# Two-layer GNN on one core: the float32 copy of hn moves from VectorE to ScalarE

## The chip, the cores and the metric

The kernel runs on one core of a Trainium2 chip. The metric is the device time of one execution in microseconds (us). The time before is 2117.98 us, the median of 3 runs (2113.94 to 2120.04).

## The reference, cut to what matters

128 independent graphs, each with features x of 128 nodes x 512 and a 128 x 128 adjacency matrix, go through two layers:

```
# layer 0, per graph
h = relu(layernorm(x));  A = adj + I;  d = rowsum(A) ** -0.5
x = x + (d A d) @ (h @ W + b)
# layer 1, per graph;  H = (adj != 0), Be = 1 / (nodes of each edge), Dn = 1 / (H @ w), w = first row of adj
xh = relu(layernorm(x))
h  = relu(Dn * (H @ (Be * (H^T @ (xh @ W1^T)))) + b1)       # 128 x 1024
hn = layernorm(h) * gamma + beta
x  = x + xh + Dn * (H @ (Be * (H^T @ (hn @ W2^T)))) + b2
```

## The kernel before, in words

Every product is done in float16 with a split: a float32 value v becomes hi = float16(v) and lo = float16(v - hi), and three matmuls (hi x hi, hi x lo, lo x hi) are added up in PSUM. Aggregation over nodes is done before the product with the weights, so each graph has five such pieces on TensorE: T0 (h0 with A), Y0 (with W), T1 (xh with P, where P = H Be H^T), Y1 in two halves of 512 columns (with W1), T2 (hn with P) and Y2 (with W2).

The work is a software pipeline written out by hand. Each engine has its own instruction stream, and `every_step` runs `step(i, k)` for k = -3 to 130; in step k an engine works on pieces of up to six neighbouring graphs (a = k, b_ = k-1, c = k-2, o = k-3, p = k+1, e = k+2). Steps 6 to 123 are a hardware loop that holds two steps in its body, so one step of two has the jump back behind it. The order within an engine is the order of the code; between engines semaphores are waited on. Most tiles have one buffer, some have two by the parity of the graph.

TensorE's order in a step: the row sums, Y1's second half (line 314, ps_c, graph c), T0 (L303 to L305, graph a; it waits for h0_hi and h0_lo), Y2 (L314, ps_y, graph o; waits for t2h and t2l), deg, T1 (graph b_), Y0, P, T2 (L303 to L305, ps_t, graph c; waits for hn_hi and hn_lo), Y1's first half (graph b_; waits for t1h and t1l), and the transpose of the next adjacency matrix.

The second layer norm of graph c: VectorE makes z from Y1's halves (L598, two instructions; the second is called z1 below), ScalarE makes h = relu(z) (L460), VectorE takes bn_stats (L603) and bn_aggr (L708), and GpSimd turns these into a scale sc2 and a bias nm2 (L930, L935, L938). Then:

```
L475 ScalarE:  hn_hi = Identity(h * sc2 + nm2)   (float16), waits for nm2
L763 VectorE:  hn    = h * sc2 + nm2             (float32), waits for nm2
L777 VectorE:  hn_lo = hn - hn_hi,                waits for both
```

ScalarE's hn_hi stands at the top of its following step, and behind it t1h (L480), which waits for T1. On VectorE hn is followed by HB_lo (L767), hn_lo (L777), out_t (L786, the finished output of graph o), t1l (L791), two tiny instructions, and the next step begins with x1 (L619). Later in that next step comes raw0 (L642, bn_stats of the next x_t, which waits for its load), t2l, the first z, u (L667), h0_lo (L673) and z1.

SyncE's queue in a step: the load of adj_t, then the store of out_t (it waits for out_t), and behind that the load of x_t for graph a+2, which raw0 of the next step reads.

GpSimd, behind nm2 (L938), goes on with base0 (L845, 128x512), qdn (L852), dn2 and dn1 (L860, L867), bias0 (L872), and scr2 (L878, 128x512, the sum of x1b and xh), and none of these waits for hn.

Of the kernel before, what the change touches and what calls it, by code (L numbers as in the profile page):

```python
# [5 lines left out]
def bass_adjacency_prenorm_two_layer_gnn_kernel(  # L6
# [24 lines left out]
    ALU = mybir.AluOpType  # L31
    ACT = mybir.ActivationFunctionType
# [30 lines left out]
    with ctx:  # L63
        def sb(name, shape, dt=F32):
            return ctx.enter_context(nc.sbuf_tensor(name, shape, dt))

        def sem(name):
            return ctx.enter_context(nc.semaphore(name))
# [58 lines left out]
        z, h = sb("z", [128, DH]), sb("h", [128, DH])  # L127
        raw2, st2 = sb("raw2", [128, NCH, 6]), sb("st2", [128, 2, 2])
        u2, sc2, nm2 = sb("u2", [128, 1]), sb("sc2", [128, 2]), sb("nm2", [128, 2])
        hn = sb("hn", [128, DH])  # L130
# [68 lines left out]
        s_h = [sem(f"h_chunk{c}_ready") for c in range(NCH)]  # L199
        s_rw2 = [sem(f"bn_raw2_chunk{c}_ready") for c in range(NCH)]  # L200
        s_stat2 = sem("stats2_ready")
        s_u2, s_pp2, s_ln2 = sem("ln2_var_eps"), sem("ln2_rstd"), sem("ln2_scalars_ready")
        s_hn, s_hnh, s_hnl = sem("hn_ready"), sem("hn_hi_ready"), sem("hn_lo_ready")
# [4 lines left out]
        def live(g, i):  # L208
            return not isinstance(i, int) or 0 <= g < NG
# [4 lines left out]
        def wait(eng, s, i, g):  # L214

            if not isinstance(i, int) or g >= 0:
                eng.wait_ge(s, i + (g + 1 if not isinstance(i, int) else min(g + 1, NG)))
# [212 lines left out]
        def _(act):  # L430
# [36 lines left out]
            def step(i, k):  # L467
                e, a, b_, c, o = k + 2, k, k - 1, k - 2, k - 3
                if live(o, i):
                    m = o % 2  # L470
                    wait(act, s_ln2, i, o)
                    wait(act, s_h[0], i, o)
                    wait(act, s_h[1], i, o)
                    wait(act, s_t2, i, o - 1)
                    act.activation(hn_hi[:, :], h[:, :], ACT.Identity, bias=nm2[:, m:m + 1], scale=sc2[:, m:m + 1])\  # L475
                       .then_inc(s_hnh, 1)
                if live(c, i):
                    wait(act, s_t1, i, c)
                    wait(act, s_y1[NCH - 1], i, c - 1)
                    act.activation(t1h[:, :], T1[:, :], ACT.Copy, scale=T1_EVAC).then_inc(s_t1h, 1)  # L480
# [12 lines left out]
                if live(b_, i):  # L493
                    m = b_ % 2
# [8 lines left out]
                if live(a, i):  # L503
                    m = a % 2
# [4 lines left out]
                                   scale=rd0[:, m, 0:1]).then_inc(s_h0, 1)  # L509
# [4 lines left out]
                                   scale=rd0[:, m, 0:1]).then_inc(s_h0h, 1)  # L514
# [12 lines left out]
                if live(b_, i):  # L527
                    m = b_ % 2
# [10 lines left out]
                if live(a, i):  # L539
                    m = a % 2  # L540
# [8 lines left out]
                if live(e, i):  # L549
                    m = e % 2  # L550
# [6 lines left out]
                if at_step(i, k, 2):  # L557
                    beta_term(0, 0)

            every_step(ENG.Activation, step)  # L560


        @block.vector
        def _(dve):
# [45 lines left out]
            def step(i, k):  # L610
                e, p, a, b_, c, o = k + 2, k + 1, k, k - 1, k - 2, k - 3
                if live(b_, i):
                    m = b_ % 2
# [7 lines left out]
                if live(p, i):  # L621
                    m = p % 2
# [6 lines left out]
                if live(p, i):  # L629
                    m = p % 2  # L630
# [9 lines left out]
                if live(p, i):  # L640
                    wait_dma(dve, s_x, i, p)
                    dve.bn_stats(raw0[:, :], x_t[:, p % 2, :]).then_inc(s_rw0, 1)  # L642
                    m = p % 2
# [19 lines left out]
                if live(p, i):  # L663
                    m = p % 2
# [15 lines left out]
                if live(b_, i):  # L680
                    m = b_ % 2
# [3 lines left out]
                if live(a, i):  # L685
                    wait(dve, s_cm, i, a)
                    dve.reciprocal(inv_t[:, :], cm[:, :]).then_inc(s_bi, 1)
                    m = a % 2
# [52 lines left out]
                if live(b_, i):  # L741
                    m = b_ % 2
# [6 lines left out]
                if live(a, i):  # L749
                    m = a % 2  # L750
# [3 lines left out]
                if live(e, i):  # L754
                    m = e % 2
# [1 line left out]
                    wait(dve, s_ahat, i, e)  # L757
                    wait(dve, s_t0, i, e - 2)
                    dve.tensor_tensor(A_lo[:, m, :], ahat[:, :], A_hi[:, m, :], ALU.subtract).then_inc(s_al, 1)
                if live(c, i):  # L760
                    m = c % 2
                    wait(dve, s_ln2, i, c)
                    dve.tensor_scalar(hn[:, :], h[:, :], sc2[:, m:m + 1], nm2[:, m:m + 1], ALU.mult, ALU.add).then_inc(s_hn, 1)  # L763
                if live(a, i):
                    m = a % 2
                    wait(dve, s_hbh, i, a)
# [13 lines left out]
                if live(o, i):  # L780
                    m = o % 2
# [11 lines left out]
                if live(e, i):  # L793
                    m = e % 2
# [5 lines left out]
                if live(p, i):  # L800
                    m = p % 2
                    wait(dve, s_ht, i, p)
                    dve.tensor_scalar(cm[:, :], cnt[:, m:m + 1], 1.0, 1.0 / P_SCALE, ALU.max, ALU.mult).then_inc(s_cm, 1)

            every_step(ENG.DVE, step)


# [168 lines left out]
```

## Time and profile before

| | us |
|---|---|
| median of 3 runs | 2117.98 |
| the profiled execution | 2120.77 |
| its span, first to last instruction | 2119.0 |
| TensorE busy (matmul) | 2066.9 |
| VectorE busy | 1852.1 |
| GpSimd busy | 1448.8 |
| ScalarE busy | 1203.7 |
| hn_hi on ScalarE, L475, mean of one | 1.241 |
| hn on VectorE, L763, mean of one | 1.287 |
| hn_lo on VectorE, L777, mean of one | 1.219 |

The span is one execution; busy times of the engines overlap. A group's mean says nothing of when its instructions run; for that the timeline is read. Start times are counted from the span's start. The granted TensorE clock had a mean of 0.995.

### The profile page before, as it was taken

The numbers are of one execution on the slowest core, as the hardware profiler recorded it, in microseconds if no ns is written. First come the engines' busy times: TensorE is split into PE (matmuls) and PEld (weight loads), VectorE is DVE, ScalarE is ACT, GpSimd is POOL, SyncE is SP. The second block draws the span as 40 slices with busy tenths as digits, with TensorE's granted clock in tenths as the row PEclk, the third lists the DMA queues.
The fourth block names the chain that finished last, engine by engine and source line by source line (L and its number), as shares of the span: only waits on it lengthen the run. The fifth ranks groups of instructions, "written<-read, shape, count | busy, mean of one in ns | idle before, by whom it ended". The sixth has DMA issues, their size and how long they took to land.

```text
span 2119.0 us, 52979 instructions
## 1 busy us (share of the span) xinstructions
PE 2066.9 (98%) x14614; PEld 1139.8 (54%) x14614; DVE 1852.1 (87%) x4514; ACT 1203.7 (57%) x2225; POOL 1448.8 (68%) x2318
## 2 busy tenths in 40 slices
PE   4899999999999999999999999999999999999998
PEld 2455555555555555555555555555555555555554
DVE  5989889888889988888888888888898898888875
ACT  6555555555555555555555555555555555555553
POOL 3667667767767767776776676776677677667663
PEclk9999999999999999999999999999999999999999
DMA  4011111110111111111111111111111111111100
GB/s 147 30 34 35 43 33 35 43 33 35 40 37 35 35 41 33 35 43 33 35 43 33 35 40 37 33 35 43 33 35 43 33 35 43 34 35 37 39 27 21
DMA packets 58346, 82.13 MB, mean 39 GB/s; under 512 B 6736, under 2 KB 23120, under 8 KB 58320
## 3 DMA queue, kind: packets, MB, share of 16 engines
q1 hardware_dynamic: 58320, 81.82, 11.9%
q8 instruction: 11, 0.18, 0.0%
q14 instruction: 15, 0.12, 0.0%
HBM read 48.24 MB, written 33.55 MB: 39 GB/s over the span
## 4 chain that ended last, share of the span: by engine, by line
PE 95%; issue 2%; DVE 1%; DMA 1%; POOL 1%; ACT 0%; SPq 0%; DVEq 0%; POOLq 0%
PE ps_c L314 46%; PE ps_y L314 31%; PE ps_c L303 3%; PE ps_c L304 3%; PE ps_c L305 3%; PE ps_t L303 3%; PE ps_t L304 3%; PE ps_t L305 3%; PE ps_a L424 1%; DMA adj_t<-in_adj_dram 0%; PE ps_p L397 0%; PE ps_p L396 0%; PE ps_y L332 0%; DMA raw_w<-in_W_dram 0%; DVE raw L603 0%
## 5 line engine op out<-in xcount | busy, mean ns | idle before, releaser
L908 POOL TENSOR_TENSOR rd<-u,neg_half 128x2 f32<-128x2 f32 x128 | 137.8, 1077 | 227.6 <-DVE u L667 227.6
L498 ACT ACTIVATE P_hi<-ps_p 128x128 f16<-128x128 f32 x128 | 35.4, 277 | 441.2 <-PE ps_t L305 433.2
L460 ACT ACTIVATE h<-z 128x512 f32<-128x512 f32 x256 | 161.3, 630 | 192.3 <-DVE z L598 192.0
L314 PE MATMUL ps_c<-w1l,t1h 128*128 128x512 f16 x1024 | 263.4, 380 | 0.0
L314 PE MATMUL ps_c<-w1h,t1h 128*128 128x512 f16 x1024 | 263.3, 379 | 0.0
L314 PE MATMUL ps_c<-w1h,t1l 128*128 128x512 f16 x1024 | 262.8, 379 | 0.0
L475 ACT ACTIVATE hn_hi<-h,nm,sc 128x1024 f16<-128x1024 f32 x128 | 158.8, 1241 | 172.0 <-POOL nm L938 171.9
L314 PE MATMUL ps_y<-w2h,t2h 128*128 128x512 f16 x1024 | 243.3, 381 | 2.4 <-issue 2.4
L598 DVE SCALAR_TENSOR_TENSOR z<-ps_c,dn,b_all 128x512 f32<-128x512 f32 x256 | 188.2, 735 | 62.8 <-PE ps_c L314 62.3
L314 PE MATMUL ps_y<-w2l,t2h 128*128 128x512 f16 x1024 | 242.3, 379 | 0.0
L891 POOL TENSOR_TENSOR x1b<-x,b_all 128x512 f32<-128x512 f32 x128 | 162.6, 1270 | 116.0 <-DVE x L619 116.0
L314 PE MATMUL ps_y<-w2h,t2l 128*128 128x512 f16 x1024 | 241.9, 379 | 0.0
L930 POOL TENSOR_SCALAR u<-st 128x1 f32<-128x1 f32 x128 | 92.9, 726 | 174.9 <-DVE st L708 174.8
L845 POOL TENSOR_TENSOR base<-scr,x_t 128x512 f32<-128x512 f32 x128 | 182.6, 1426 | 27.0 <-issue 22.4
L763 DVE TENSOR_SCALAR hn<-h,sc,nm 128x1024 f32<-128x1024 f32 x128 | 164.7, 1287 | 25.1 <-POOL nm L938 25.1
L303 PE MATMUL ps_t<-P_hi,hn_hi 128*128 128x128 f16 x1024 | 178.2, 219 | 4.9 <-issue 4.2
L305 PE MATMUL ps_t<-P_hi,hn_lo 128*128 128x128 f16 x1024 | 178.3, 219 | 0.0
L304 PE MATMUL ps_t<-P_lo,hn_hi 128*128 128x128 f16 x1024 | 178.3, 219 | 0.0
L826 POOL TENSOR_TENSOR base<-scr,vq 128x512 f32<-128x512 f32 x128 | 162.8, 1272 | 11.4 <-ACT vq L454 11.4
L314 PEld LDWEIGHTS ps_c<-w1l,t1h 128*128 128x128 f16 x1024 | 100.3, 98 | 121.5 <-issue 1.1
L314 PEld LDWEIGHTS ps_y<-w2l,t2h 128*128 128x128 f16 x1024 | 100.4, 98 | 121.4 <-issue 1.1
L314 PEld LDWEIGHTS ps_c<-w1h,t1l 128*128 128x128 f16 x1024 | 100.2, 98 | 121.0 <-issue 0.3
(133 smaller groups left out, 5774.1 us busy)
## 6 DMA issues: line engine op xcount, KB each, us to landing
x_t<-in_x_dram SPq DMA_DIRECT2D x128, 256.0 KB, 2.7
out_dram<-out_t SPq DMA_DIRECT2D x128, 256.0 KB, 2.0
adj_t<-in_adj_dram SPq DMA_DIRECT2D x128, 64.0 KB, 1.8
raw_w<-in_W1T_dram SPq DMA_DIRECT2D x4, 512.0 KB, 7.6
raw_w<-in_W2T_dram SPq DMA_DIRECT2D x8, 256.0 KB, 8.8
raw_w<-in_W_dram SPq DMA_DIRECT2D x4, 256.0 KB, 3.7
b_all<-in_b_dram SPq DMA_DIRECT2D x2, 256.0 KB, 6.9
b_all<-in_b_dram SPq DMA_DIRECT2D x1, 512.0 KB, 10.3
```

Of the source, the lines that this page charges most:

```text
L303: pe.matmul(ps[:, f], lhs_hi[:, f], rhs_hi, start=True, stop=False)
L304: pe.matmul(ps[:, f], lhs_hi[:, f], rhs_lo, start=False, stop=False)
L305: mm = pe.matmul(ps[:, f], lhs_lo[:, f], rhs_hi, start=False, stop=True)
L314: mm = pe.matmul(ps, t[:, j * 128:(j + 1) * 128], w[:, j, cols], start=(n == 0 and j == 0), stop=(n == 2 and j == blocks - 1))
L460: act.activation(h[:, cols], z[:, cols], ACT.Relu).then_inc(s_h[n], 1)
L475: act.activation(hn_hi[:, :], h[:, :], ACT.Identity, bias=nm2[:, m:m + 1], scale=sc2[:, m:m + 1])\
L598: dve.scalar_tensor_tensor(out=z[:, cols], in0=Y1[n][:, :], scalar=dn1[:, m:m + 1], in1=b1_all[:, cols], op0=ALU.mult, op1=ALU.add).then_i ...
L763: dve.tensor_scalar(hn[:, :], h[:, :], sc2[:, m:m + 1], nm2[:, m:m + 1], ALU.mult, ALU.add).then_inc(s_hn, 1)
L826: pool.tensor_tensor(base2[:, m, :], scr2[:, m, :], vq[:, :], ALU.add).then_inc(s_base2, 1)
L845: pool.tensor_tensor(base0[:, :], scr0[:, :], x_t[:, a % 2, :], ALU.add).then_inc(s_base0, 1)
L891: pool.tensor_tensor(x1b[:, :], x1[:, a % 2, :], b2_all[:, :], ALU.add).then_inc(s_x1b, 1)
L908: pool.tensor_tensor(rd0[:, m, :], u0[:, m, :], neg_half[:, :], ALU.pow).then_inc(s_pp0, 1)
```

## The change

The VectorE instruction for hn is taken out. ScalarE makes hn with the same function, scale and bias as hn_hi, as one more instruction right behind hn_hi. It has the waits of hn_hi, but for the last: where hn_hi waits for T2 of the graph before, hn waits for hn_lo of the graph before, the reader of the single buffer. Everything else keeps its order.

```diff
@@ ScalarE, top of the step @@
                     act.activation(hn_hi[:, :], h[:, :], ACT.Identity, bias=nm2[:, m:m + 1], scale=sc2[:, m:m + 1])\
                        .then_inc(s_hnh, 1)
+                    wait(act, s_ln2, i, o)
+                    wait(act, s_h[0], i, o)
+                    wait(act, s_h[1], i, o)
+                    wait(act, s_hnl, i, o - 1)
+                    act.activation(hn[:, :], h[:, :], ACT.Identity, bias=nm2[:, m:m + 1], scale=sc2[:, m:m + 1])\
+                       .then_inc(s_hn, 1)
                 if live(c, i):
                     wait(act, s_t1, i, c)
@@ VectorE, behind A_lo @@
-                if live(c, i):
-                    m = c % 2
-                    wait(dve, s_ln2, i, c)
-                    dve.tensor_scalar(hn[:, :], h[:, :], sc2[:, m:m + 1], nm2[:, m:m + 1], ALU.mult, ALU.add).then_inc(s_hn, 1)
                 if live(a, i):
                     m = a % 2
                     wait(dve, s_hbh, i, a)
```

## Rows read from the trace of the kernel before

**Rows 1.** The page, part 1: busy us (share of the span) and instructions.
```profile
PE 2066.9 (98%) x14614; PEld 1139.8 (54%) x14614; DVE 1852.1 (87%) x4514; ACT 1203.7 (57%) x2225; POOL 1448.8 (68%) x2318
```

**Rows 2.** Windows from one step's T0 to another's, 119 steps on: length, busy.
```profile
106.52:2013.44 1906.92, 1903.88 (x13567) 1051.82 (x13566) 1703.62 (x4165) 1094.49 (x2023) 1342.53 (x2142) 1.00 0.11 37
```

**Rows 3.** Timeline of TensorE: start, length in us; first matmuls of T0 and T2.
```profile
1004.10 0.22 PE L303 MATMUL ps_c<-A_hi,h_hi 128*128 128x128 f16 x1
...
1013.34 0.22 PE L303 MATMUL ps_t<-P_hi,hn_hi 128*128 128x128 f16 x1
...
1020.02 0.22 PE L303 MATMUL ps_c<-A_hi,h_hi 128*128 128x128 f16 x1
...
1036.03 0.22 PE L303 MATMUL ps_c<-A_hi,h_hi 128*128 128x128 f16 x1
```

**Rows 4.** Waits: who waited for whom, us in total, times, longest.
```profile
DVE raw L642 <- DMA x_t<-in_x_dram: 56.1, 68, 1.1
```

**Rows 5.** Timeline of VectorE over two steps; idle before in brackets.
```profile
1004.05 0.75 DVE L598 SCALAR_TENSOR_TENSOR z<-ps_c,dn,b_all 128x512 f32<-128x512 f32 x1 [0.21 <-PE ps_c L314]
...
1008.85 1.74 DVE L763 TENSOR_SCALAR hn<-h,sc,nm 128x1024 f32<-128x1024 f32 x1 [0.17 <-POOL nm L938]
...
1010.79 1.21 DVE L777 TENSOR_TENSOR hn_lo<-hn,hn_hi 128x1024 f16<-128x1024 f32 x1
...
1020.23 0.75 DVE L598 SCALAR_TENSOR_TENSOR z<-ps_c,dn,b_all 128x512 f32<-128x512 f32 x1 [0.72 <-PE ps_c L314]
...
1027.04 1.21 DVE L777 TENSOR_TENSOR hn_lo<-hn,hn_hi 128x1024 f16<-128x1024 f32 x1
1028.17 0.74 DVE L786 SCALAR_TENSOR_TENSOR out_t<-ps_y,dn,base 128x512 f32<-128x512 f32 x1
...
1032.36 0.69 DVE L642 BATCH_NORM_STATS2 raw<-x_t 128x6 f32<-128x512 f32 x1 [0.78 <-DMA x_t<-in_x_dram]
...
1035.08 0.69 DVE L673 TENSOR_TENSOR h_lo<-h,h_hi 128x512 f16<-128x512 f32 x1
```

**Rows 6.** Timeline of SyncE's queue: the two loads of x_t.
```profile
1013.43 0.33 SPq L246 DMA_DIRECT2D x_t<-in_x_dram  x1
...
1029.78 0.33 SPq L246 DMA_DIRECT2D x_t<-in_x_dram  x1
```

**Rows 7.** The page, part 6: issues, KB each, median us to landing.
```profile
x_t<-in_x_dram SPq DMA_DIRECT2D x128, 256.0 KB, 2.7
```

**Rows 8.** Timeline of ScalarE in these steps, and one row near the end.
```profile
1008.93 1.24 ACT L475 ACTIVATE hn_hi<-h,nm,sc 128x1024 f16<-128x1024 f32 x1 [1.36 <-POOL nm L938]
...
1016.10 0.81 ACT L508 ACTIVATE h<-x_t,bias,rd 128x512 f32<-128x512 f32 x1
1016.81 0.81 ACT L513 ACTIVATE h_hi<-x_t,bias,rd 128x512 f16<-128x512 f32 x1
...
1025.02 1.24 ACT L475 ACTIVATE hn_hi<-h,nm,sc 128x1024 f16<-128x1024 f32 x1 [1.28 <-POOL nm L938]
...
2087.45 1.24 ACT L475 ACTIVATE hn_hi<-h,nm,sc 128x1024 f16<-128x1024 f32 x1 [2.65 <-POOL nm L938]
```

**Rows 9.** Timeline of GpSimd in these steps, and one row near the end.
```profile
1008.78 1.26 POOL L845 TENSOR_TENSOR base<-scr,x_t 128x512 f32<-128x512 f32 x1
...
1025.37 1.60 POOL L845 TENSOR_TENSOR base<-scr,x_t 128x512 f32<-128x512 f32 x1 [0.38 <-issue]
1027.06 1.32 POOL L852 TENSOR_SCALAR qdn<-q,dn 128x1 f32<-128x1 f32 x1
...
1028.99 1.27 POOL L878 TENSOR_TENSOR scr<-x1b,xh 128x512 f32<-128x512 f32 x1
...
2088.67 1.26 POOL L878 TENSOR_TENSOR scr<-x1b,xh 128x512 f32<-128x512 f32 x1
```

**Rows 10.** One line of the program, L852: duration ns min/median/max.
```profile
L852 POOL TENSOR_SCALAR qdn<-q,dn x128: 288/590/1323, 43.4 to 2087.5; 128x1 f32<-128x1 f32 x128
```

**Rows 11.** Timeline of VectorE near the end, beside the last rows of 8 and 9.
```profile
2088.78 2.24 DVE L777 TENSOR_TENSOR hn_lo<-hn,hn_hi 128x1024 f16<-128x1024 f32 x1 [0.52 <-ACT hn_hi L475]
```

## The prediction

> **What bounds the kernel now.** I read the busy times first: TensorE 98%, VectorE 87%, ScalarE 57% [rows 1]. That says "TensorE", but not how near VectorE stands behind it. So next the steps: 119 of them take 1906.92 us [rows 2], 16.02 each, 32.05 for two. In the timeline T0 starts at 1004.10, 1020.02 and 1036.03 [rows 3]: 15.92 is what TensorE needs for a step with nothing to wait for, 9.24 of it from T0 to T2 and 6.68 from T2 to the next T0. Only about 0.1 us a step is lost. The loss sits at T0: in the second step h0_lo ends at 1035.77 and T0 starts 0.27 later, while z1, which needs only the matmuls ahead of T0, starts 0.21 behind T0 where T0 isn't held (1020.23 against 1020.02) [rows 3, 5].
>
> Why is h0_lo late? VectorE waits for x_t ahead of raw0 in every second step (68 waits) [rows 4], and x_t is loaded behind the store of out_t, and out_t stands behind hn_lo. The chain from one step to the next, in the second step: z1 1020.23, hn_lo 1027.04 to 1028.25, out_t to 1028.91 (+0.66), issue of x_t 1029.78 (+0.87; +0.77 in the first step, 1013.43), raw0 1032.36, h0_lo to 1035.77 (+3.41), T0 1036.03 [rows 3, 5, 6]. Landing takes 2.7 in the median [rows 7]. So hn_lo, which the change touches, already stands on the path that sets T0, with almost no slack. I call the step of 1008 A and that of 1025 B; they alternate.
>
> **The change part by part.**
>
> Removed: hn on VectorE, which took 1.74 in A (it stood behind base0, which started at 1008.78 and ended at 1010.04) [rows 5, 9]. The time freed is ahead of hn_lo, and VectorE has nothing to put there but HB_lo, so it turns into waiting for ScalarE. Worth nothing by itself.
>
> Added: a second pass on ScalarE. No row has Identity with a float32 result at this size; the same form with float32 and with float16 results takes 0.81 both ways and the second starts 0.71 after the first [rows 8], so I take 1.24 as for hn_hi, 0.10 of it overlapped. Bounds: 0.81 (as a 512-wide one) and 1.5. VectorE starts 0.09 after ScalarE's end (2087.45 + 1.24 = 2088.69, then 2088.78) [rows 8, 11]. So hn_lo can start in A at 1008.93 + 1.14 + 1.24 + 0.08 = 1011.39 (was 1010.79, +0.60), in B at 1025.02 + 2.46 = 1027.48 (was 1027.04, +0.44) [rows 5, 8]. The waits added are met by then. Behind hn on ScalarE stands t1h, some 0.4 to 0.5 later than before; its reader t1l stands two VectorE instructions behind hn_lo, which is later still, so that costs nothing.
>
> Moved by that, the large term: hn_lo meets scr2 on GpSimd. Near the end, scr2 started at 2088.67 and hn_lo at 2088.78, and hn_lo took 2.24 instead of 1.21: it ended 1.09 after scr2's end [rows 9, 11]. The reverse is seen as well: qdn took 1.32 beside hn_lo in B [rows 5, 9] and 0.29 where nothing is beside it [rows 10]. So the two exclude each other, and the first to start wins. Where does scr2 stand in the changed kernel? In A base0 ends at 1010.04, qdn starts 0.10 later and now needs 0.29 (hn_lo is not yet there): 1010.43. From qdn's end to scr2's start B shows 0.61 (1028.38 to 1028.99). So scr2 starts at 1011.04, or up to 0.09 later if HB_lo gets in ahead of base0; hn_lo comes at 1011.39, 0.26 to 0.35 too late, and ends 1.09 behind scr2's end at about 1012.36: 1013.45 instead of 1012.00. In B base0 starts 0.38 later (the jump back): 1025.37 + 1.26 + 0.09 + 0.29 + 0.61 = 1027.62 for scr2, and hn_lo comes at 1027.48, ahead of it by 0.14, with bias0 in front for a moment; I take its end at 1028.75 (was 1028.25).
>
> The steps then, counted from z1's start. A: hn_lo ends 9.40 after z1 (1013.45 - 1004.05); +0.66 +0.77 +2.70 +3.41 puts h0_lo's end at 16.93. VectorE's z1 of the next step stands behind it: 16.86. T0 of B is at 16.93 + 0.27 = 17.20, 0.34 behind its z1. B: hn_lo ends at 8.52; +0.66 +0.87 +2.70 +3.41 = 16.16, T0 could start at 16.43; TensorE itself allows z1 at 0.34 + 15.92 + 0.21 = 16.47, which is later. Pair: 16.86 + 16.47 = 33.33 against 32.05, +1.28. T2 waits too in A (natural 9.20, hn_lo ready 9.66), but the longer chain covers it. 59.5 pairs give +76; the last graph, with no work beside it, adds the second pass, 1.1. On the profiled execution: 2120.8 + 77 = 2198. That execution is 2.8 above the median of the runs, so 2195.
>
> A rule about those ports: the Trainium skill, "SBUF — State Buffer", "Who interferes with whom", has the shared pair of VectorE and GpSimd as a lock held for the whole instruction by the one that issues first. The 2.24 us agrees. For nm2 it makes a difference: HB_lo now follows A_lo directly, while nm2 runs. By the page nm2, issued first, isn't held and the sum stays; qdn's median of 0.59 over its 0.29 [rows 10] says that a tiny GpSimd instruction can lose 0.30 beside HB_lo. If nm2 loses 0.25 in each step, A's chain is longer by that: +15 us, 2210. I keep it inside the range.
>
> **The rivals.**
>
> 1. No collision: hn_lo starts ahead of scr2 in both steps (the second pass shorter by 0.3, or GpSimd's small instructions slower). Then only +0.60 and +0.44 remain: h0_lo + 0.27 at 16.36 after z1 in both, plus 15.92 + 0.21 back to z1: 32.47 to 32.49 a pair, +0.43, 26 us with the end: 2144. Against it: the 0.26 to 0.35 margin in A is a sum of rows.
>
> 2. Collision in both: B's margin of 0.14 fails. hn_lo ends at 1027.62 + 1.27 + 1.09 = 1029.98, 9.75 after z1; h0_lo ends at 17.39, z1 of the next A at 17.32: 34.18 a pair, +2.13, 127 us: 2245.
>
> 3. Faster: VectorE at 87% is the near bottleneck, it loses 1.29 us a step (mean of L763), and T0's waits vanish. The 1906.92 become 119 x 15.92 = 1894.5, 12 us less: 2106. It is decided where h0_lo is bound by VectorE's queue and not by x_t's load; it would need hn ready by 1010.79, a second pass of under 0.7 us. Rows 4 and the 0.78 wait at 1032.36 [rows 5] speak against it. The Trainium skill, "Perfetto Trace Analysis", "Optimizing Scalar/DVE Operations", says that moving work to ScalarE may make sense if VectorE is saturated; that rule would give this rival. The trace shows it short of saturated where it counts: it waits.
>
> 4. No change: the delay of hn_lo is swallowed, because out_t's store or the load has slack that the chain of waits hides: 2112 to 2124. For it: in A raw0 shows no wait for x_t. Against it: B does, in nearly every pair.
>
> **How the numbers follow.** Collision in A alone 0.62 (own range 2175 to 2216, for landings of 2.6 to 2.8, nm2's 0.25 and bounds of the pass); none 0.15; both 0.12; faster 0.06; no change 0.05. The likeliest gives 2195. The range for 8 in 10 takes in rival 1 and the lower part of what lies towards rival 2: 2140 to 2228. 0.3% is 6.4 us, about what a measurement can tell from no change: faster 0.06, same 0.05, slower 0.89.
>
> **What would show it.** L475 has 256 instructions or L481 stands beside it with 1.24 each; hn_lo (mean 1.22 before) has two kinds, 1.2 in B and about 2.1 in A, where scr2 starts first; base0 falls to 1.26 in both; raw0 waits for x_t in every step, some 0.5 in A and about as much in B; T0 starts at intervals near 17.2 and 16.1 in turn; VectorE's busy share falls by the 1.29 a step less what hn_lo gains; TensorE's busy time stays. I am wrong if hn_lo stays at 1.2 throughout (rival 1), if it is over 2 throughout (rival 2), or if T0's intervals stay at 15.9 and 16.1.

## The result: 2256 us, slower by 6.5%

| | us |
|---|---|
| before, median of 4 runs | 2119.01 (2113.94 to 2121.32) |
| after, median of 4 runs | 2256.34 (2256.04 to 2257.04) |
| ratio, 95% interval | 1.0651 (1.0635 to 1.0667) |
| span of the profiled execution, before and after | 2119.0 and 2254.2 |

The direction was forecast, the size was not: 2195 with a range of 2140 to 2228 stood against 2256. It is the second rival, the collision in both steps, that came out (2245 was worked out for it). Lines have moved: hn_lo is L779, hn L481, nm2 L940, scr2 L880, raw0 L648, h0_lo L679 and z L604 in the changed kernel.

### The profile after

The page's busy times and two groups of instructions (line, engine, operation, busy us and mean ns, idle time ahead and its releaser).

```profile
PE 2102.3 (93%) x14614; PEld 1140.5 (51%) x14614; DVE 1724.0 (76%) x4386; ACT 1334.2 (59%) x2353; POOL 1420.3 (63%) x2318
...
L779 DVE TENSOR_TENSOR hn_lo<-hn,hn_hi 128x1024 f16<-128x1024 f32 x128 | 276.0, 2157 | 324.9 <-ACT hn L481 324.9
...
L648 DVE BATCH_NORM_STATS2 raw<-x_t 128x6 f32<-128x512 f32 x128 | 88.7, 693 | 132.9 <-DMA x_t<-in_x_dram 132.9
```

VectorE did not simply lose 1.29 us a step: hn_lo's mean grew from 1.22 to 2.16, which is 120 us of being held over 128 steps, and 325 us of idle time ahead of hn_lo are new. The load of x_t is now waited for in 122 steps (68 in [rows 4]), for 133 us in all. The same 119 steps as in [rows 2], by windows:

```profile
110.20:2143.21 2033.01, 1933.01 (x13567) 1050.02 (x13567) 1584.63 (x4047) 1215.26 (x2143) 1318.45 (x2143) 1.00 0.11 35
```

2033.01 / 119 = 17.08 a step, 34.17 a pair, where it was 16.02 and 32.05. These steps carry 126.1 of the 135.2 us by which the span grew; filling and draining the pipeline carry the other 9. The clock is granted in full (1.00), so this isn't the clock.

The timeline of VectorE, a step A (from 1066.92) and a step B (from 1083.88); start, length, in brackets the idle time before.

```profile
1066.92 0.75 DVE L604 SCALAR_TENSOR_TENSOR z<-ps_c,dn,b_all 128x512 f32<-128x512 f32 x1
...
1071.26 0.28 DVE L765 TENSOR_TENSOR A_lo<-ahat,A_hi 128x128 f16<-128x128 f32 x1
1071.46 0.34 DVE L769 SCALAR_TENSOR_TENSOR HB_lo<-H_T,inv_t,HB_hi 128x128 f16<-128x128 f16 x1
1074.38 2.03 DVE L779 TENSOR_TENSOR hn_lo<-hn,hn_hi 128x1024 f16<-128x1024 f32 x1 [2.57 <-ACT hn L481]
...
1080.56 0.69 DVE L648 BATCH_NORM_STATS2 raw<-x_t 128x6 f32<-128x512 f32 x1 [1.09 <-DMA x_t<-in_x_dram]
...
1083.28 0.68 DVE L679 TENSOR_TENSOR h_lo<-h,h_hi 128x512 f16<-128x512 f32 x1
1083.88 0.74 DVE L604 SCALAR_TENSOR_TENSOR z<-ps_c,dn,b_all 128x512 f32<-128x512 f32 x1
...
1091.26 2.35 DVE L779 TENSOR_TENSOR hn_lo<-hn,hn_hi 128x1024 f16<-128x1024 f32 x1 [2.49 <-ACT hn L481]
```

z1 at 1083.88 has no wait for TensorE any more ([rows 5] have 0.21 and 0.72): it follows h0_lo directly. So a ring that begins and ends on VectorE sets the step: z1, nm2 on GpSimd, hn on ScalarE, hn_lo, out_t, the load of x_t, h0_lo and z1 again. The timeline of GpSimd in the same steps:

```profile
1071.37 0.49 POOL L940 TENSOR_SCALAR nm<-st,sc 128x1 f32<-128x1 f32 x1 [0.17 <-POOL sc L937]
1071.82 1.27 POOL L847 TENSOR_TENSOR base<-scr,x_t 128x512 f32<-128x512 f32 x1
...
1074.06 1.26 POOL L880 TENSOR_TENSOR scr<-x1b,xh 128x512 f32<-128x512 f32 x1
...
1088.33 0.49 POOL L940 TENSOR_SCALAR nm<-st,sc 128x1 f32<-128x1 f32 x1 [0.17 <-POOL sc L937]
1089.02 1.27 POOL L847 TENSOR_TENSOR base<-scr,x_t 128x512 f32<-128x512 f32 x1 [0.20 <-issue]
...
1091.04 0.27 POOL L874 TENSOR_SCALAR bias<-st,rd 128x1 f32<-128x1 f32 x1
1091.26 1.27 POOL L880 TENSOR_TENSOR scr<-x1b,xh 128x512 f32<-128x512 f32 x1
```

In A scr2 starts at 1074.06 and hn_lo 0.32 later, as worked out (0.26 to 0.35). In B both start at 1091.26, the margin of 0.14 is gone, and hn_lo takes 2.35. It starts while bias0 (1091.04 to 1091.31) still runs, and scr2, the next of GpSimd, goes ahead of it. The margin went into nm2: 0.49 instead of 0.31, because HB_lo (1071.46 in A) now runs beside it. hn on ScalarE follows nm2's end and comes 0.18 later; base0 in B does not: it starts 0.69 behind nm2's start (1088.33 to 1089.02), where it was 0.70 with nm2 at 0.31, and its idle time ahead shrank from 0.38 to 0.20. The profile calls that idle time "issue" and names no cause; nm2 is the last instruction of GpSimd's step and base0 the first of the next, so in one step of two the loop's jump back stands between them, and that it is the cause is my reading. The pass itself took the time that was assumed (ScalarE, step A):

```profile
1071.97 1.24 ACT L475 ACTIVATE hn_hi<-h,nm,sc 128x1024 f16<-128x1024 f32 x1 [1.54 <-POOL nm L940]
1073.12 1.23 ACT L481 ACTIVATE hn<-h,nm,sc 128x1024 f32<-128x1024 f32 x1
```

### The profile page after: what moved, and what is told of

Same layout as the page of the kernel before. It is cut to its first block, busy times and chain, and to the rows that moved or that the text cites. A ratio compares the mean times of both kernels' runs of the same rounds, so it can differ in the third digit from the quotient of the medians.

```text
span 2254.2 us, 53234 instructions
## 1 busy us (share of the span) xinstructions
PE 2102.3 (93%) x14614; PEld 1140.5 (51%) x14614; DVE 1724.0 (76%) x4386; ACT 1334.2 (59%) x2353; POOL 1420.3 (63%) x2318
## 4 chain that ended last, share of the span: by engine, by line
issue 30%; DVE 25%; DMA 14%; POOL 10%; ACT 7%; PE 5%; SPq 3%; DVEq 2%; POOLq 1%; ACTq 0%
DMA x_t<-in_x_dram 14%; ACT hn L481 7%; DVE raw L609 6%; DVE out_t L788 4%; DVE z L604 4%; POOL u L932 4%; DVE raw L648 4%; POOL sc L937 3%; POOL nm L940 3%; SPq L278 2%; PE ps_c L314 2%; PE ps_y L314 2%; DVEq L217 2%; DVE st L714 1%; DVE P_lo L690 1%
## 5 line engine op out<-in xcount | busy, mean ns | idle before, releaser
L779 DVE TENSOR_TENSOR hn_lo<-hn,hn_hi 128x1024 f16<-128x1024 f32 x128 | 276.0, 2157 | 324.9 <-ACT hn L481 324.9
L604 DVE SCALAR_TENSOR_TENSOR z<-ps_c,dn,b_all 128x512 f32<-128x512 f32 x256 | 187.4, 732 | 6.3 <-PE ps_c L314 6.3
L648 DVE BATCH_NORM_STATS2 raw<-x_t 128x6 f32<-128x512 f32 x128 | 88.7, 693 | 132.9 <-DMA x_t<-in_x_dram 132.9
L303 PE MATMUL ps_c<-A_hi,h_hi 128*128 128x128 f16 x512 | 93.2, 220 | 95.2 <-DVE h_lo L679 92.3
L847 POOL TENSOR_TENSOR base<-scr,x_t 128x512 f32<-128x512 f32 x128 | 162.8, 1272 | 15.9 <-issue 11.7
L880 POOL TENSOR_TENSOR scr<-x1b,xh 128x512 f32<-128x512 f32 x128 | 163.5, 1277 | 0.0
L609 DVE BATCH_NORM_STATS2 raw<-h 128x6 f32<-128x512 f32 x256 | 163.3, 678 | 0.1
```

The source lines that it names most:

```text
L303: pe.matmul(ps[:, f], lhs_hi[:, f], rhs_hi, start=True, stop=False)
L604: dve.scalar_tensor_tensor(out=z[:, cols], in0=Y1[n][:, :], scalar=dn1[:, m:m + 1], in1=b1_all[:, cols], op0=ALU.mult, op1=ALU.add).then_i ...
L609: dve.bn_stats(raw2[:, n, :], h[:, n * CH:(n + 1) * CH]).then_inc(s_rw2[n], 1)
L779: dve.tensor_tensor(hn_lo[:, :], hn[:, :], hn_hi[:, :], ALU.subtract).then_inc(s_hnl, 1)
L847: pool.tensor_tensor(base0[:, :], scr0[:, :], x_t[:, a % 2, :], ALU.add).then_inc(s_base0, 1)
L880: pool.tensor_tensor(scr2[:, b_ % 2, :], x1b[:, :], xh[:, :], ALU.add).then_inc(s_scr2, 1)
```

## The experiments

Times are medians. The kernel before ran beside them: 2120.26 is the median of its 7 runs beside e1 to e4, 2117.57 that of its 16 runs beside e5 to e8. Ratios are to the kernel before, as they are on record, and can differ in the third decimal from a quotient of two medians of this table. The last column is the time from the sixth T0 to the 125th, over 119; for the kernel before it is that of [rows 2].

| | us | ratio, 95% interval | us a step |
|---|---|---|---|
| before, beside e1 to e4 | 2120.26 | | 16.02 |
| before, beside e5 to e8 | 2117.57 | | 16.02 |
| after | 2256.34 | 1.0651 (1.0635 to 1.0667) | 17.08 |
| e1: scr2 waits for hn_lo | 2157.14 | 1.0183 (1.0166 to 1.0200) | 16.32 |
| e2: HB_lo behind nm2 | 2196.59 | 1.0363 (1.0345 to 1.0380) | 16.61 |
| e3: both | 2146.84 | 1.0134 (1.0117 to 1.0150) | 16.24 |
| e4: hn not made at all | 2104.70 | 0.9932 (0.9911 to 0.9953) | 15.93 |
| e5: before, x_t's load first | 2108.91 | 0.9957 (0.9944 to 0.9971) | 15.93 |
| e6: after, x_t's load first | 2207.57 | 1.0418 (1.0401 to 1.0434) | 16.72 |
| e7: e3 with x_t's load first | 2110.84 | 0.9967 (0.9955 to 0.9980) | 15.93 |
| e8: before, second pass added | 2116.80 | 0.9999 (0.9990 to 1.0008) | 16.01 |

**e1: take the collision away.**

```diff
@@ GpSimd, scr2 @@
                     wait(pool, s_base2, i, b_ - 2)
+                    wait(pool, s_hnl, i, c)
                     pool.tensor_tensor(scr2[:, b_ % 2, :], x1b[:, :], xh[:, :], ALU.add).then_inc(s_scr2, 1)
```

> Edit: GpSimd's scr2 also waits for hn_lo of the same step, the rest as in the changed kernel. Theory (hn_lo is blocked by scr2 in both steps, 2.03 and 2.35 us instead of 1.21): hn_lo falls to 1.21, and ends 8.67 and 8.59 after z1 instead of 9.49 and 9.73; h0_lo is then 16.47 to 16.49 behind z1 with TensorE's 0.27, a pair takes 32.6 instead of 34.2, and the median falls from 2256 to about 2155. nm2 stays at 0.49. Rival (the loss is the second pass on ScalarE itself, its place in the queue or its latency): less than a quarter of the loss comes back, over 2220.

Measured 2157.1 against about 2155 expected: 99 of the 137 us come back by one wait on an engine that had nothing to do with hn. The first two lines are of the timeline of VectorE and GpSimd in a step B, the last is nm2 of that step:

```profile
1209.27 1.22 DVE L779 TENSOR_TENSOR hn_lo<-hn,hn_hi 128x1024 f16<-128x1024 f32 x1 [2.49 <-ACT hn L481]
...
1210.67 1.27 POOL L881 TENSOR_TENSOR scr<-x1b,xh 128x512 f32<-128x512 f32 x1 [1.39 <-DVE hn_lo L779]
...
1206.34 0.49 POOL L941 TENSOR_SCALAR nm<-st,sc 128x1 f32<-128x1 f32 x1 [0.17 <-POOL sc L938]
```

hn_lo still waits 2.49 for ScalarE, but takes 1.22; nm2 keeps its 0.49.

**e2: give nm2 its 0.31 back, leave scr2.**

```diff
@@ VectorE, ahead of HB_lo @@
+                    wait(dve, s_ln2, i, c)
                     wait(dve, s_hbh, i, a)
                     dve.scalar_tensor_tensor(out=HB_lo[:, :], in0=H_T[:, m, :], scalar=inv_t[:, :], in1=HB_hi[:, :],
```

> Edit: VectorE waits for nm2 ahead of HB_lo, as it did when hn stood there; the rest as in the changed kernel. Theory (HB_lo held nm2 up by 0.18, which took the margin of 0.14 in step B away): nm2 falls from 0.49 to 0.31, hn_lo starts ahead of scr2 in B and takes 1.2 to 1.3 there, and stays at 2.0 to 2.1 in A; that is the kernel that the prediction described: 2195, 2180 to 2215. Rival (B collides whatever nm2 does, since bias0 is in front of hn_lo and scr2 follows it): B stays at 2.2 or more, and the median only falls by what nm2 gives directly, 0.18 a step or less, to 2235 to 2250.

Measured 2196.6, where the prediction gave 2195 for a collision in A alone; T0 starts at intervals of 17.21 and 16.03 in turn (medians), where it said 17.2 and 16.1. Timeline of VectorE and GpSimd, a step A and then a step B:

```profile
1211.78 2.04 DVE L780 TENSOR_TENSOR hn_lo<-hn,hn_hi 128x1024 f16<-128x1024 f32 x1 [1.14 <-ACT hn L481]
...
1228.33 1.23 DVE L780 TENSOR_TENSOR hn_lo<-hn,hn_hi 128x1024 f16<-128x1024 f32 x1 [2.06 <-ACT hn L481]
...
1211.46 1.27 POOL L881 TENSOR_TENSOR scr<-x1b,xh 128x512 f32<-128x512 f32 x1
...
1225.58 0.31 POOL L941 TENSOR_SCALAR nm<-st,sc 128x1 f32<-128x1 f32 x1 [0.17 <-POOL sc L938]
1228.28 1.32 POOL L875 TENSOR_SCALAR bias<-st,rd 128x1 f32<-128x1 f32 x1
1229.57 1.26 POOL L881 TENSOR_TENSOR scr<-x1b,xh 128x512 f32<-128x512 f32 x1
```

With nm2 at 0.31 hn_lo in B starts ahead of scr2, takes 1.23, and scr2 comes behind it at 1229.57. A stays at 2.04, scr2 0.32 ahead. So 0.18 us of a 128x1 instruction decided 60 us. One thing is not as it was described: in B bias0 did not stand in front of hn_lo. It is recorded 0.05 ahead of it (1228.28 and 1228.33), but it is bias0 that was held, 1.32 instead of 0.27, in nearly every step B. In e3, where bias0 is recorded 0.06 ahead (1202.63 and 1202.69), it takes 0.26 and hn_lo 1.27. So hn_lo won the place ahead of GpSimd's row of small instructions in e2 by a few hundredths of a microsecond, and which of two so close goes first can't be read from their starts.

**e3: both edits.**

> Edit: both of the above on the changed kernel. Theory: only the second pass is left of the change, hn_lo ends 8.55 and 8.47 behind z1, a pair takes 32.47, the median is 2144 (2138 to 2152). Rival (the second pass costs nothing once GpSimd is out of the way): 2119. Rival (it costs its full 1.14 in each step): 2119 + 119 x 1.14 = 2255.

Measured 2146.8, where 2144 was expected: what is left is the second pass, and it acts through x_t's load alone (e7 shows that). e1 less e3 is 10 us: each chain of two steps runs through nm2 once, and 59.5 x 0.18 = 11.

**e4: the removal without the addition.** hn isn't computed; hn_lo is made from h, which leaves the normalisation out of its operand. The edit against the changed kernel, without the lines that put other waits in the place of those for hn:

```diff
@@ ScalarE, behind hn_hi; its four waits go too @@
-                    act.activation(hn[:, :], h[:, :], ACT.Identity, bias=nm2[:, m:m + 1], scale=sc2[:, m:m + 1])\
-                       .then_inc(s_hn, 1)
@@ VectorE, hn_lo @@
-                    wait(dve, s_hn, i, c)
                     wait(dve, s_hnh, i, c)
                     wait(dve, s_t2, i, c - 1)
-                    dve.tensor_tensor(hn_lo[:, :], hn[:, :], hn_hi[:, :], ALU.subtract).then_inc(s_hnl, 1)
+                    dve.tensor_tensor(hn_lo[:, :], h[:, :], hn_hi[:, :], ALU.subtract).then_inc(s_hnl, 1)
```

> Edit: hn isn't made at all, on neither engine; hn_lo reads h in its place (so the normalisation is left out of hn_lo's operand), and what waited for hn waits for hn_hi and hn_lo. This is the removal without the addition. Theory: hn_lo starts 1.24 + 0.1 behind nm2, ends about 7.6 behind z1 (7.95 and 8.02 in the kernel before), T0 is no longer held by x_t, a step is TensorE's own 15.92: 2105 to 2110. VectorE's 1.29 us less a step is worth no more than that. Rival (VectorE's queue was no bound at all, not even by x_t): 2119 as before.

Measured 2104.7. Taking 1.29 us a step off an engine that was 87% busy, at no price, is worth 16 us of the 165 (2120.26 less 2104.70). The steps go at 15.93 (106.39 to 2001.67 for 119), so 12 of them are T0's waits. Of the two profiled spans another 3 us of difference lie behind the 125th T0; hn_lo has little work beside it there, but that this is the reason was not tested.

**e5: the load of x_t ahead of the store, in the kernel before.**

```diff
@@ SyncE, in the step, behind load_adj @@
-                if live(o, i):
-                    wait(sp, s_out, i, o)
-                    sp.dma_start(out[bass.ds(i + o, 1), :, :].rearrange("g n f -> n (g f)"), out_t[:, o % 2, :])\
-                      .then_inc(s_st[o % 2], 16)
                 if not isinstance(i, int) or 0 <= a < NG - 2:
                     wait(sp, s_h0, i, a)
                     wait(sp, s_h0h, i, a)
                     wait(sp, s_base0, i, a)
                     load_x(i, a + 2)
+                if live(o, i):
+                    wait(sp, s_out, i, o)
+                    sp.dma_start(out[bass.ds(i + o, 1), :, :].rearrange("g n f -> n (g f)"), out_t[:, o % 2, :])\
+                      .then_inc(s_st[o % 2], 16)
```

> Edit: in the kernel before, SyncE issues the load of x_t ahead of the store of out_t. Theory (in every second step T0 waits for h0_lo, that for x_t's load, that for out_t behind hn_lo): the waits of raw0 for x_t vanish, T0's intervals are 15.92 throughout, 119 x 0.1 = 12 us less: 2105 to 2110. Rival (T0's wait has another cause, VectorE's own queue): no change, 2119.

Measured 2108.9, under both kernels, and against the kernel before by more than the interval. raw0 waits for no load in any step, and from the sixth T0 to the 125th it is 107.53 to 2002.80, 15.93 a step: TensorE's own time to within 0.01. VectorE is as full as before (87%).

**e6: the same swap in the changed kernel.**

> Edit: the same swap in the changed kernel. Theory: raw0 no longer waits for x_t, but hn_lo ends 9.49 and 9.73 behind z1 as before, and T2 then waits for it: z1 to z1 is 0.21 + hn_lo's end + 0.27 + 6.68 = 16.65 and 16.89, together 33.54 a pair instead of 34.17: 2256 - 38 = 2218. Rival (x_t's load is the only path that carries the delay): the swap gives all back, about 2110.

Measured 2207.6, 10 under what was expected; the pair took 33.44 against 33.54. x_t's load is not the only path. With it gone TensorE waits at T2, which reads hn_lo (timelines of VectorE and GpSimd, then of TensorE):

```profile
1204.17 2.36 DVE L779 TENSOR_TENSOR hn_lo<-hn,hn_hi 128x1024 f16<-128x1024 f32 x1 [2.49 <-ACT hn L481]
...
1204.18 1.27 POOL L880 TENSOR_TENSOR scr<-x1b,xh 128x512 f32<-128x512 f32 x1
```

```profile
1206.78 0.22 PE L303 MATMUL ps_t<-P_hi,hn_hi 128*128 128x128 f16 x1 [0.79 <-issue]
1213.46 0.22 PE L303 MATMUL ps_c<-A_hi,h_hi 128*128 128x128 f16 x1
1223.36 0.22 PE L303 MATMUL ps_t<-P_hi,hn_hi 128*128 128x128 f16 x1 [0.50 <-issue]
1230.04 0.22 PE L303 MATMUL ps_c<-A_hi,h_hi 128*128 128x128 f16 x1
```

T2 is held for 0.79 and 0.50 ("issue": the profile names no releaser, but hn_lo ends at 1204.17 + 2.36 = 1206.53, and T2 starts 0.25 behind it); T0 is 6.68 behind T2, so it isn't held.

**e7: e3 with the swap.**

> Edit: the swap, scr2 behind hn_lo, and HB_lo behind nm2, all in the changed kernel. Theory: hn_lo ends 8.5 behind z1, T2's natural place is 9.03 behind it, 0.2 of slack left: nothing holds TensorE, 15.92 a step, 2105 to 2112, the same as the kernel before with the swap. Rival (the freed VectorE time is worth something once the ports and x_t are out of the way): clearly under 2105.

Measured 2110.8, 15.93 a step like e5. hn on ScalarE then costs nothing in these steps, and the freed time of VectorE (80% busy) brings nothing either.

**e8: the second pass alone.**

```diff
@@ kernel before, ScalarE, behind hn_hi @@
+                    act.activation(hn_x[:, :], h[:, :], ACT.Identity, bias=nm2[:, m:m + 1], scale=sc2[:, m:m + 1])\
+                       .then_inc(s_hnx, 1)
```

(the waits that guard the tile and its inputs are as for hn in the changed kernel)

> Edit: the kernel before with the second pass added on ScalarE into a tile of its own that nobody reads; VectorE makes hn as before. Theory (ScalarE has the room; only hn_lo's waiting for the pass costs): t1h comes 0.4 to 0.5 later in each step and nothing waits for it: 2119 (2115 to 2123). Rival (the second pass holds up t1h, then t1l and Y1): 30 us or more on top.

Measured 2116.8, ratio 0.9999 (0.9990 to 1.0008). The page has ScalarE at 1334.1 us busy, as in the changed kernel, and t1h starts 2.28 behind hn_hi's start, 1.91 in the kernel before (1010.84 after [rows 8]' 1008.93):

```profile
1008.01 1.24 ACT L477 ACTIVATE hn_hi<-h,nm,sc 128x1024 f16<-128x1024 f32 x1 [1.36 <-POOL nm L947]
1009.15 1.23 ACT L483 ACTIVATE hn_x<-h,nm,sc 128x1024 f32<-128x1024 f32 x1
1010.29 0.57 ACT L488 ACTIVATE t1h<-ps_c 128x512 f16<-128x512 f32 x1
```

ScalarE had the room. What costs is that hn_lo has to wait for the end of the pass.

## Why the prediction was wrong

The step that failed is the place of hn_lo in B, "hn_lo comes at 1027.48, ahead of it by 0.14, with bias0 in front for a moment". In the changed kernel hn_lo came level with scr2, was held, and took 2.35 instead of the 1.27 of the sum. The terms around it, one by one:

- The bound. That T0 waits for h0_lo, that for x_t's load, and that for out_t behind hn_lo, is shown by e5: change the order of the two transfers alone, and the step falls from 16.02 to 15.93.
- The removal, put at nothing by itself. In a kernel where hn_lo waits for ScalarE it is worth nothing (e7 beside e5). By itself it isn't: with nothing added in its place (e4) hn_lo starts earlier, T0's waits go, and 16 us are gained.
- The second pass. 1.23 us, 1.15 behind hn_hi's start (1.24 and 1.14 were taken). By itself, with both collisions gone, it costs 27 us (e3), against 26 in the sum of rival 1.
- The collision in A. hn_lo 0.32 behind scr2's start, 2.03 to 2.04 long; with scr2 kept behind it (e1, e3) it takes 1.2 to 1.3. e2 less e3 is 50 us.
- The sum for its case. e2, where only A collides, takes 2196.6 and 33.23 a pair; 2195 and 33.33 were worked out. That the total is nearer than the pairs (0.10 a pair too long is 6 us) is luck: the filling and draining, where more was lost than the sum has, made up for it.
- nm2. The text saw that HB_lo now runs beside nm2, put it at up to 0.25, and priced it at 15 us as a length alone. It is 0.18 and by length costs 10 (e1 less e3). But it also moves hn_lo against scr2, whose start in B does not follow nm2, and the margin there was 0.14. That was not carried over. A possible delay of 0.25 stood against a margin of 0.14, in two paragraphs that were never held beside each other. Put together they make rival 2 more than a case of 0.12. Besides, hn_lo was taken to go between bias0 and scr2. In B of the changed kernel, where bias0 already ran when hn_lo came, scr2 went next and hn_lo behind it, in all such steps but one; where hn_lo went first (e2), it was ahead of bias0 too.
- The rule on the lock. By the Trainium skill, "SBUF — State Buffer", "Who interferes with whom", the pair goes to the one that issues first, and so nm2 would not be held by HB_lo. But it took longer in nearly every step (median 490 ns, 313 before). The measurement decides: nm2's start is recorded at 1071.37, 0.09 ahead of HB_lo's, and it still took 0.49; with HB_lo put behind it (e2) it took 0.31. That both stood behind A_lo (1071.26 to 1071.54) and HB_lo was let in first is my reading, and no row shows the order within.

The steps that rival 2 had worked out came to 34.18 a pair, and 34.17 was measured. So near is luck in part: it has 16.86 for A and 17.32 for B, and the trace has 16.93 and 17.27 on average. A is longer since there scr2 follows nm2's end and nm2's 0.18 is not in rival 2's sum. Rival 2's total, 2245, is 11 under the 2256. About 8 of these are the filling and draining: 1.1 was taken for them, and they cost 9, of which 3.7 lie ahead of the sixth T0 and 5.4 behind the 125th. Those stretches hold steps that slow down as well, and the 59.5 pairs leave them out; the sum of the likeliest case has the same gap.

From 2119 to 2256 in parts, by the runs: the second pass by its latency 27 (e3), the collision in A 50 (e2 less e3), and nm2's 0.18 with the collision in B that it brings 60 (after less e2), of which about 10 is nm2's length. Each difference of medians from separate sets of runs is uncertain by some 3 us, as the medians of the kernel before are (2117.57 to 2120.26). That B's collision alone is 50 is a difference of those and has no run of its own.

## What to carry to other kernels

An engine that is 87% busy is no bound while it waits for something else in every second step; ask what the instruction moved was standing ahead of, and which transfer is queued behind that one's result. When work leaves one of two engines that block each other, every later pair of their instructions meets at new times: list the margins, and compare each with the sum of all the small delays ahead of it, not with one. And where a load stands in a queue behind a store that waits for a result, put the load first: here that alone was worth more (2108.9) than moving the work.

## What the runs showed of the hardware

- Recorded starts don't say which of two instructions that exclude each other goes first. hn_lo started with scr2 (1091.26 both) and even 0.01 ahead of it (e6: 1204.17 and 1204.18), and took 2.35 and 2.36 instead of 1.21, both times until 1.08 behind scr2's end. And bias0, recorded 0.05 ahead of hn_lo, was held by it in e2 (1.32), but recorded 0.06 ahead in e3 it went first (0.26).
- A GpSimd instruction recorded as started 0.09 ahead of a VectorE one can still be held by it: nm2 0.49 beside HB_lo, 0.31 without.
- Across GpSimd's jump back a longer instruction ahead of it cost nothing: base0 starts 0.69 behind nm2's start in step B with nm2 at 0.49, and 0.70 behind it with nm2 at 0.31; the idle time shown ahead of it fell from 0.38 to 0.20.
